# A decoder block on one core: the warm-up matmuls between the attention units and the first gate product are taken out

## The reference

```python
# self-attention with relative positions, 16 heads of 8
xn = layernorm(x) * gamma + beta
q, k, v = xn @ Wq.T + bq, xn @ Wk.T + bk, xn @ Wv.T + bv
score = ((q + u_bias) @ k.T + rel_shift((q + v_bias) @ (pos_emb @ Wpos.T).T)) / sqrt(8)
x = layernorm(x + softmax(score) @ v @ Wout.T + bout)
# cross-attention on 77 context rows, no weights
x = layernorm(x + softmax(x @ ctx.T) @ ctx)
# mixture of 16 experts (F = 64), best two of each token, and a shared one (F = 128)
shared = silu(x @ Sg) * (x @ Su) @ Sd
routed = sum over e of cw[:, e] * (silu(x @ Wg[e]) * (x @ Wu[e]) @ Wd[e])   # cw: softmax share of the best two, else 0
x = layernorm(x + routed + shared)
```

## Time and profile before

| | us |
|---|---|
| median of 3 runs | 154.34 |
| lowest, highest | 153.58, 154.52 |
| profiled execution, its own time | 152.93 |
| its span, first to last instruction | 151.1 |
| TensorE matmuls busy | 138.6 (92%) |
| TensorE weight loads busy | 104.6 (69%) |
| VectorE busy | 116.8 (77%) |
| GpSimd busy | 98.5 (65%) |
| ScalarE busy | 91.2 (60%) |
| mean granted TensorE clock | 0.988 of full |

### The profile page before, as it was taken

The page is one execution under the profiler, slowest core; times in us unless marked ns, Lnnn a source line. Parts: engine busy times, 40 slices in busy tenths (PEclk is TensorE's granted clock), DMA queues, the critical chain, the costliest instruction groups (busy, mean ns, idle before and its releaser), DMA issues.

```text
span 151.1 us, 5091 instructions
## 1 busy us (share of the span) xinstructions
PE 138.6 (92%) x2079; PEld 104.6 (69%) x2079; DVE 116.8 (77%) x339; ACT 91.2 (60%) x184; POOL 98.5 (65%) x115
## 2 busy tenths in 40 slices
PE   6999999998999999887999999999999999999940
PEld 2453668776889999875647677766777886676930
DVE  5969579899999997999629989884756999666062
ACT  3678635996998868398880333776765335566100
POOL 8795893579875688279495533534799517951932
PEclk9999999999999999999999999999999999999995
DMA  4590133200144810000005000000000000100001
GB/s 147 166 314 1 35 83 84 57 0 4 41 106 91 221 23 7 4 4 2 4 0 162 33 4 0 0 0 0 4 0 2 2 0 0 39 35 0 0 0 69
DMA packets 5465, 6.59 MB, mean 44 GB/s; under 512 B 1051, under 2 KB 4611, under 8 KB 5315
## 3 DMA queue, kind: packets, MB, share of 16 engines
q1 hardware_dynamic: 4867, 5.75, 13.6%
q10 hardware_dynamic: 576, 0.53, 1.1%
HBM read 3.79 MB, written 0.52 MB: 29 GB/s over the span
## 4 chain that ended last, share of the span: by engine, by line
PE 58%; DVE 23%; ACT 8%; issue 4%; DMA 2%; POOL 2%; POOLq 1%; DVEq 0%; ACTq 0%
PE ps L907 55%; DVE pm L749 7%; ACT ph L579 2%; ACT moe_c L575 2%; DVE st L672 2%; DMA x_sb<-in_x 2%; PE ps L1015 2%; DVE nmx L768 2%; DVE pm L756 2%; DVE nm L771 2%; ACT q_c L505 2%; DVE q_c L715 1%; POOL pl L453 1%; DVE nm L775 1%; DVE mv L675 1%
## 5 line engine op out<-in xcount | busy, mean ns | idle before, releaser
L453 POOL TENSOR_TENSOR pl<-moe_c,ph 128x1024 f16<-128x1024 f32 x16 | 34.1, 2132 | 13.4 <-ACT ph L579 13.4
L462 POOL TENSOR_TENSOR ph<-ph 128x512 f32<-128x512 f32 x16 | 20.4, 1284 | 10.9 <-ACT ph L646 5.8
L907 PEld LDWEIGHTS ps<-qd,kp 128*128 128x128 f16 x768 | 23.5, 98 | 3.7 <-issue 1.4
L907 PE MATMUL ps<-qd,kp 128*128 128x32 f16 (+1 forms) x768 | 25.0, 193 | 1.1 <-ACT ph L579 0.7
L749 DVE TRANSPOSE_TENSOR_REDUCE pm<-ps 128x32 f32<-128x1024 f32 x16 | 20.0, 1249 | 3.2 <-PE ps L907 2.9
L575 ACT ACTIVATE moe_c<-ps 128x1024 f32<-128x1024 f32 x16 | 16.6, 1037 | 5.1 <-PE ps L907 4.9
L907 PE MATMUL ps<-moe_c,ph 128*128 128x128 f32 x144 | 19.0, 280 | 0.1
L907 PEld LDWEIGHTS ps<-moe_c,ph 128*128 128x128 f32 x144 | 17.5, 191 | 2.1 <-issue 1.6
L579 ACT ACTIVATE ph<-ps 128x1024 f16<-128x1024 f32 x16 | 16.5, 1033 | 0.0
L818 DVE SCALAR_TENSOR_TENSOR ph<-ph,ps 128x512 f32<-128x512 f32 x18 | 12.2, 677 | 5.6 <-ACT ph L637 5.6
L907 PEld LDWEIGHTS ps<-i,nm 128*128 128x128 bf16 x512 | 14.2, 96 | 2.7 <-DVE nm L775 2.1
(11 more groups left out here) (137 smaller groups left out, 269.4 us busy)
## 6 DMA issues: line engine op xcount, KB each, us to landing
qd<-q_dn SPq DMA_DIRECT2D x28, 64.0 KB, 2.5
ph<-in_w_ffn SPq DMA_DIRECT2D x1, 1152.0 KB, 5.2
moe_c<-in_w_down SPq DMA_DIRECT2D x1, 576.0 KB, 4.1
x_sb<-in_x SPq DMA_DIRECT2D x2, 256.0 KB, 3.4
out<-pl SPq DMA_DIRECT2D x4, 128.0 KB, 1.8
wp<-in_w_proj ACTq DMA_DIRECT2D x1, 320.0 KB, 4.5
kp_c<-in_ctx_t SPq DMA_DIRECT2D x1, 308.0 KB
cn<-in_ctx_n SPq DMA_DIRECT2D x1, 308.0 KB
```

The costliest lines, as they stand in the source:

```text
L453: nc.gpsimd.tensor_tensor(lo, p32[:, u % 2, :].rearrange("p (n i) -> p n i", i=CI), hi, ALU.subtract).then_inc(p_lo, 1)
L462: nc.gpsimd.tensor_tensor(hh[:, k % 3, :], gu[:, k % 3, :], cwr[:, k % 3, :], ALU.mult).then_inc(hid_ready, 1)
L907: return nc.tensor.matmul(o, w, r, start=start, stop=stop, skip_group_check=True)
```

## The change

The ten `warm` steps in TensorE's table go, and with them the branch that carries them out and the constant of their bank. The 18 matmuls at the start stay, and all other tables and steps are as they were.

```diff
-            pv2 scores13 ctxT0 pv3 shift11 shift12 attn0 ctxT1 scores14 attn1 shift13 scores15 norm0 warm2 cross0
-            warm3 shift14 norm1 probs0 warm2 shift15 warm2 cross1 warm6 mix0 probs1 warm2 mix1 pv4 pv5 warm3 next0
-            warm3 pv6 lg0 pv7 next1 warm3 lg1 warm2 gate_up0 gate_up1 ctxT2 ctxT3 attn2 attn3 gate_up2 down0 cwT0
+            pv2 scores13 ctxT0 pv3 shift11 shift12 attn0 ctxT1 scores14 attn1 shift13 scores15 norm0 cross0
+            shift14 norm1 probs0 shift15 cross1 mix0 probs1 mix1 pv4 pv5 next0
+            pv6 lg0 pv7 next1 lg1 gate_up0 gate_up1 ctxT2 ctxT3 attn2 attn3 gate_up2 down0 cwT0
...
-        WARM_BANK = 2
...
-                elif stage == "warm":
-                    late = reader[WARM_BANK] is not None
-                    pe.wait_ge(p_hi, UNITS if late else UNITS - 2)
-                    for _ in range(n):
-                        mm(ps[:, 0 if late else WARM_BANK, :], i_warm[:, 0:P], i_warm[:, :], True, True)
```

## The result

The changed kernel takes 156.95 us (median of 4 runs, 156.25 to 157.18); the kernel before, run beside it, 153.96 us (4 runs). The ratio is 1.019, with a 95% interval of 1.0128 to 1.0252. That is slower by 3.0 us where +1.3 against the median was forecast: inside the range, but on the far side of the 1%, to which the forecast gave 0.37. The profiled execution took 156.25 us with a span of 154.5, against 152.93 and 151.1 before. Medians here are over all executions of a kernel, while a ratio and its interval leave out executions more than 1.5% above the fastest of their kernel, so that a ratio is not quite the quotient of the two medians.

A forecast was written before the change was run, and what follows sets the result against it. From 77.86 us TensorE steps with short hand-overs bound the kernel, from 87.64 TensorE alone. 152.93 - 0.1 (warm-ups) + 1.4 (low clock) = 154.2 us; with the runs' median 1.41 above the profiled one, forecast 155.6, range 153.8 to 158.0.

The forecast's parts named there:

- its own case: Clock falls once or twice between 72 and 88 us and rises in between; cost 0.2 to 3 us, chance 0.55.
- low until the gate products: Rival: clock stays low from first cross score product to about 90 us; 157.8 us, up to 160.6, chance 0.13.
- Term 1: Time of the 28 removed warm-up matmuls, lying under waits in ten groups: between 0 and -0.2 us, taken as -0.1.
- The rival that they held real steps back: Warm-ups, not the semaphore, cause the ten hand-overs of up to 0.15 us; 1.5 us won, 152.8 us, chance 0.05.
- Up to 77.8 us a low clock costs almost nothing: Changed stretch up to 77.8 us: ScalarE paces it and TensorE's steps have slack, so almost no cost.
- Prices at the low level: Low-clock costs from 77.86 us on: fp32 steps +2.0, attention outputs +0.4, gate and up matmuls +1.2; +3.6 if low throughout.
- the doubling that stood as the upper bound: Narrow matmuls of the four second-half attention outputs taking twice as long at low clock: +3.2 us, against +0.4 taken.
- How long the clock is low: Between 72 and 88 us, one or two falls with a rise in between; +1.4 us of the +3.6 for low throughout.
- the first two kinds of steps: From 77.86 us: fp32 products and transposes (+2.0) and four attention outputs (+0.4) if low throughout; a third taken, +0.8.
- the third: Gate and up matmuls from 87.64 us: 0.21 us more each at low clock, six bounding it at +1.2; half taken, +0.6.
- the two terms: The warm-up matmuls' own time, -0.1 us, and TensorE's low clock after the change, +1.4 us.
- The rival that the clock stays up: Clock does not fall in the thinned stretch, whose longest opened idle time is 1.6 us; 154.2 us, chance 0.25.

## Why the prediction was right, and where it was small

The forecast was +1.3 us, the measured change +3.0. The loss, 3.0 us by the medians and 3.2 by the profile, stands at the end of the 0.2 to 3 us that the prediction allowed its own case, and 156.95 us is nearer to the 157.8 of the rival "low until the gate products", which had a chance of 0.13, than to the forecast's 155.6. The kind of cost and its place were foreseen, its size was not: that the number lies in the range is due to a range wide enough for that rival too.

**Term 1, the warm-ups themselves (-0.1 us): right.** Halving them changed the time by a factor of 1.0001 and moved none of the steps in the table by more than 0.03 us, so the gain is zero within what can be measured; doubling them showed that they lie just under their waits. The rival that they held real steps back is out.

**Up to 77.8 us a low clock costs almost nothing: right in the changed kernel.** Low from 72.6 to 75.9, and 0.09 us lost at the first mix product.

**Prices at the low level: right.** Gate and up matmuls stand 0.43 us apart (89.79 to 90.22), as taken from the start of the program. (There the clock row reads nine all the same, so the low level of the start shows in durations alone.) The first and the last of the 64 matmuls of two attention outputs in the changed kernel's timeline:

```profile
80.70 0.21 PE L906 MATMUL ps<-vp,ph 128*128 128x34 f16 x1
...
82.51 0.19 PE L906 MATMUL ps<-vp,pl 128*128 128x34 f16 x1
```

(82.51 - 80.70) / 63 = 0.029 us, which is the value scaled from the wide matmuls; the doubling that stood as the upper bound is out. The Trainium skill's estimate of 28 ns (TensorE: Matmul & The Clock Gate, "Back-to-back issue gap") agrees. (An attention output has 32 such matmuls, not the 64 that the prediction names; its 1.6 us for two outputs, and the sum, go by 32.) The fp32 steps grew by 1.6 to 1.7: the second mix product 0.66 to 1.12, transposes 0.41 to 0.66, router products 0.59 to 1.00. VectorE shows how such a step reaches the chain: in the kernel before it began the second mixing at 80.14 without waiting; in the changed one it stood idle for it:

```profile
80.80 0.17 DVE L863 RECIPROCAL r<-r 128x2 f32<-128x2 f32 x1 [0.41 <-PE ps L906]
```

**How long the clock is low: the step that was mis-sized.** The forecast took a third of the first two kinds of steps (+0.8) and half of the third (+0.6), because, so I thought, work at the low level takes longer and would bring the clock back in between. It did so once, at 75.9 us. From 79.4 on it did not, for 13.6 us: the first two kinds cost 1.47 us, and the gate and up matmuls 1.75 us instead of 0.6. Even the bound for the third was low: I took as many low matmuls as at the start, six (+1.2); nine ran low in the changed kernel and twelve with the first six groups. The argument behind the share failed: from 79.4 to 89.2 us the low level did fill TensorE to 74 to 85% (3.06 of 3.60, 2.46 of 3.00, 2.37 of 3.20 us), and the clock stayed low. With 1.47 and 1.75 in place of 0.8 and 0.6 the two terms give +3.2 (+3.1 with term 1), the measured 3.2 to 3.3 us of the profile. The rival "low until the gate products" had nearly the right place, only that the clock came back for one piece in between, and nearly the right price (+3.5).

**The rival that the clock stays up: wrong.** The longest idle time of TensorE shortly ahead of the first fall is 0.74 us (before `norm0`), and 1.58 us ahead of the second; both are shorter than the 2.2 us without any matmul that stood behind the fall in the trace of before. With six groups kept it fell too, behind steps with no gap over 0.71 us: thin work was enough. The Trainium skill's tie of the fall to idle gaps (TensorE: Matmul & The Clock Gate, "Why this matters for your kernels") does not cover this.

## What to carry to other kernels

Filling under waits is worth what the next dense stretch would lose at the low clock, so keep it up to that stretch: half a remedy that stopped short of it was no better than none here (1.028 against 1.019). Begin it ahead of the thin work: filling that runs at the low level takes up to twice as long and overruns its wait (0.6 us with the last four groups, 1.4 in the profile with the last six). Size it by the wait: half was enough, double cost 5.2 us. When you price a low clock, don't count on the same thin work to bring it back.

## What the runs showed of the hardware

The clock fell soon and came back late. It fell behind a stretch in which TensorE was busy for 0.90 of 2.00 us, with no gap over 0.74 us; in another run, with the first six groups kept, TensorE was busy without idle time from 88.5 us, and the level was 0.50 until 95.3. And where the fall comes, and whether it comes, differs between executions of one kernel (mean clocks of 0.965 and 0.996 with the last six groups), so one profile of such a kernel does not show its time.
